# Flamingo layer on one core: the last key tile's two key-sum additions of each head group move from GpSimd to VectorE, and the written orders of all five engines are laid anew

## The reference, cut to what matters

```
xn = layernorm(x)
Q = xn Wq' + bq;  K = ctx Wk' + bk;  V = ctx Wv' + bv          (16 heads of 32)
attn = softmax(Q K' / sqrt(32)) per head;  x1 = x + tanh(g0) (attn V Wo' + bo)
n = layernorm(x1);  probs = softmax(n Rw + rb);  gate = max probs; e = argmax probs  (8 experts)
out = x1 + tanh(g1) * gate * (n Expert[e] + expert_bias[e])
```

## Time and profile before

| | us |
|---|---|
| median of 3 runs | 1189.92 (1188.95 to 1192.12) |
| the profiled execution, its own time | 1192.07 |
| its span, first to last instruction | 1190.3 |
| PE busy / DVE busy / POOL busy / ACT busy | 1094.6 / 759.0 / 667.2 / 563.0 |
| mean granted clock | 0.956 |

### The profile page before, as it was taken

One profiled execution on the slowest core, in us unless ns is written; L12 is line 12 of the kernel. 1 busy time (PEld: TensorE's weight loads), 2 busy tenths in 40 slices (PEclk: granted clock), 3 DMA queues, 4 the chain that ended last, 5 costly groups with the idle time before them and its releaser, 6 DMA issues.

```text
span 1190.3 us, 19122 instructions
## 1 busy us (share of the span) xinstructions
PE 1094.6 (92%) x5464; PEld 709.2 (60%) x5464; DVE 759.0 (64%) x1620; ACT 563.0 (47%) x1016; POOL 667.2 (56%) x446
## 2 busy tenths in 40 slices
PE   2798999999999999999999999999999996898996
PEld 1564467556755675567556655575557642786774
DVE  4645545766576657665765677556765665778654
ACT  4145643564356435644564356445644456423431
...
GB/s 230 62 77 102 82 72 80 113 80 81 79 121 80 81 77 119 82 79 89 111 79 72 79 120 72 73 80 111 86 81 73 83 53 321 127 95 147 166 140 54
DMA packets 70885, 119.39 MB, mean 100 GB/s; under 512 B 17854, under 2 KB 18878, under 8 KB 70656
## 3 DMA queue, kind: packets, MB, share of 16 engines
...
q10 hardware_dynamic: 2048, 0.53, 0.2%
...
## 4 chain that ended last, share of the span: by engine, by line
PE 68%; DVE 13%; issue 6%; ACT 5%; POOL 3%; DMA 3%; DVEq 1%; ACTq 0%; SPq 0%; POOLq 0%
PE jb L459 10%; PE jb L460 9%; PE jb L461 9%; PE sc L482 8%; PE jb L502 8%; PE hb L492 8%; DVE maxima L836 6%; PE sc L664 5%; ACT probs L688 3%; PE jb L602 2%; PE jb L515 2%; POOL psum_keys L1095 2%; PE jb L530 1%; PE jb L594 1%; PE hb L650 1%
## 5 line engine op out<-in xcount | busy, mean ns | idle before, releaser
L836 DVE TENSOR_REDUCE maxima<-jb 128x1 f32<-128x512 f32 x512 | 321.7, 680 | 112.2 <-PE jb L502 110.8
L688 ACT ACTIVATE probs<-sc 128x512 f32<-128x512 f32 x512 | 285.4, 598 | 190.5 <-PE sc L482 153.8
L1095 POOL TENSOR_TENSOR psum_keys<-psum_keys,probs 128x1024 f32<-128x1024 f32 x128 | 302.6, 2384 | 110.7 <-ACT probs L688 110.6
L1095 POOL TENSOR_TENSOR psum_keys<-probs 128x1024 f32<-128x1024 f32 x64 | 151.8, 2383 | 231.3 <-ACT probs L688 230.9
L502 PE MATMUL jb<-k_stack,q_stack 96*128 96x512 f32 x512 | 188.4, 435 | 19.1 <-issue 4.9
L482 PE MATMUL sc<-q_stack,k_stack 98*128 98x512 f32 x512 | 190.7, 435 | 14.9 <-ACT probs L688 11.5
L482 PEld LDWEIGHTS sc<-q_stack,k_stack 98*128 98x128 f32 x512 | 94.4, 192 | 107.6 <-ACT probs L688 56.0
L502 PEld LDWEIGHTS jb<-k_stack,q_stack 96*128 96x128 f32 x512 | 92.6, 190 | 110.4 <-issue 51.2
L492 PE MATMUL hb<-probs,values 128*32 128x512 f32 x1024 | 139.3, 628 | 3.4 <-ACT probs L688 2.5
L459 PE MATMUL jb<-c_hi,wk_hi 128*128 128x512 f32 x128 | 52.4, 409 | 15.4 <-POOL c_lo L1099 15.4
L664 PE MATMUL sc<-e_hi,heads_hi 128*128 x156 | 65.9, 422 | 0.5 <-DVE heads_raw L1067 0.5
...
## 6 DMA issues: line engine op xcount, KB each, us to landing
k_stack<-k_hi SPq DMA_DIRECT2D x256, 64.0 KB, 2.0
q_stack<-q_hi SPq DMA_DIRECT2D x256, 64.0 KB, 2.0
stage<-in_x SPq DMA_DIRECT2D x63, 256.0 KB, 2.9
stage<-in_ctx_t SPq DMA_DIRECT2D x32, 256.0 KB, 3.0
k_stack<-k_lo SPq DMA_DIRECT2D x128, 64.0 KB, 2.0
q_stack<-q_lo SPq DMA_DIRECT2D x128, 64.0 KB, 2.0
e_lo<-in_ew SPq DMA_DIRECT2D x8, 1024.0 KB, 14.0
...
```

The source lines that it names most:

```text
L688: nc.scalar.activation(probs[:, kt % 2, h, :], scs[(16 * g + n) % NSC][:], ACT.Exp, scale=SCALE)\
L836: nc.vector.tensor_reduce(maxima[g % 2][:, n:n + 1], jbs[j][:], AX.X, ALU.max).then_inc(s["mx_done"], 1)
L1095: nc.gpsimd.tensor_tensor(psum_keys[:, two, :], in0, probs[:, kt % 2, two, :], ALU.add)\
```

## The change

The two additions `A4` and `A5` of each of the 32 groups leave GpSimd's table and stand in VectorE's (64 additions of 128x1024 elements in all). The semaphore `acc_done`, which counted a group's six additions, becomes two, `acc_done0` and `acc_done1`, one for each pair of heads, with three counts a group; every wait on it is rewritten to the same data. All tables are written anew. The code part, cut:

```diff
 # tensor_program, SUM
-                    pe.wait_ge(s["acc_done"], 6 * (g + 1))
+                    for i in range(2):
+                        pe.wait_ge(s[f"acc_done{i}"], 3 * (g + 1))
 # scalar_program, E
-                    wait(act, s["acc_done"], 6 * g + (h2 + 1 if kt >= 2 else 2 * kt - 4 + h2 + 1))
+                    wait(act, s[f"acc_done{h2}"], 3 * g + (1 if kt >= 2 else kt - 1))
 # vector_program, A (kt is 3 for A4 and A5)
-                    wait(dve, s["acc_done"], 6 * g + n - 1)
-                    nc.vector.tensor_tensor(psum_keys[:, two, :], psum_keys[:, two, :], probs[:, kt % 2, two, :], ALU.add)\
-                        .then_inc(s["acc_done"], 1)
+                    if kt == 1:
...
+                    else:
+                        wait(dve, s[f"acc_done{h2}"], 3 * g + kt - 1)
+                        in0 = psum_keys[:, two, :]
+                    nc.vector.tensor_tensor(psum_keys[:, two, :], in0, probs[:, kt % 2, two, :], ALU.add)\
+                        .then_inc(s[f"acc_done{h2}"], 1)
 # gpsimd_program, A
-                        wait(pool, s["acc_done"], 6 * g + n - 1)
+                        wait(pool, s[f"acc_done{h2}"], 3 * g + kt - 1)
```

The parts of the tables that the prediction speaks of:

```diff
 OPENING
 "SP"
-        "LW1 ^DC0 ^DC1 ^DC2 LW0 ^DC3 ^DX0 LC LW2 LW3 ^DX1 ^DX2 ^DX3 ^0SK ~RW2 ~RW3 ^0SQ",
+        "^DC0 ^DC1 ^DC2 LW1 ^DC3 ^DX0 LW0 ^DX1 ~RW2 ^DX2 LC ~RW3 ^DX3 LW2 LW3 ^0SK ^0SQ ^1SQ",
 "PE"
-        "^0K ^0Kb ^0Kc ^0Kd ^T4 ^T5 ^T6 ^T7 ^0Q ^0Qb ^0Qc ^0Qd ^0M0 ^0M1 ^0M2 ^0M3 ^0M4 ^0M5 ^V0 ^Vb0 ^1Q ^1Qb",
+        "^0K ^0Kb ^0Kc ^T4 ^0Kd ^T5 ^T6 ^T7 ^0Q ^0Qb ^0Qc ^0Qd ^0M0 ^0M1 ^0M2 ^0M3 CS ^0M4 ^0M5 ^0M6 ^1Q ^1Qb ^1Qc",
 "ACT"
-        "WT0 WT1 WT2 WT3 ^C0 ^C1 TH WT4 ^C2 WT5 ^C3 ^0K ^NX0 WT6 WT7 WT8 WT9 ^T4 WT10 ^NX1 WT11 WT12 ^NX2 ^T5 ^NX3",
-        "WT13 WT14 ^T6 ^T7 WT15 ^0Q ^1Q ^V0 ^0MT ^1K ^0MD ^V1 ^0E0 ^0E1 ^V2 ^0E2 ^0E3 ^0E4 ^0E5 ^0E6 ^0E7 ^0E8 ^2Q",
+        "^C0 ^C1 ^C2 WT0 WT1 WT2 WT3 ^C3 ^NX0 WT4 WT5 ^0K WT6 ^NX1 ^T4 ^NX2 ^T5 ^T6 ^NX3 ^T7 WT7 WT8 WT9 WT10 WT11",
+        "WT12 WT13 WT14 TH ^0Q WT15 ^1Q ^V0 ^0MT ^0MD ^1K ^0E0 ^0E1 ^0E2 ^V1 ^0E3 ^0E4 ^0E5 ^V2 ^0E6 ^2Q ^0E7 ^0E8",
 "DVE"
-        "WT0 WT1 WT2 ^LX0 WT3 WT4 WT5 ^LX1 ^0K ^LX2 ^LX3 ^T4 ^T5 ^T6 ^T7 WT6 WT7 WT8 WT9 WT10 ^0Q ^0M0 ^0M1 ^0M2",
+        "WT0 WT1 WT2 WT3 ^LX0 ^LX1 WT4 WT5 ^LX2 ^LX3 ^T4 ^0K ^T5 ^T6 ^T7 WT6 WT7 WT8 WT9 WT10 ^0Q WT11 WT12 WT13",
 ORDER
 "ACT" (around the start of group 3's exponentials)
-        "~RT3 2E15 3MT 3MD ~RS1 ^0K 2OU 3E0 3E1 3E2 3E3 3E4 2SUM
+        ~RT3 3MT 3MD 3E0 3E1 3E2 ^0K 2OU 3E3 3E4 3E5 2SUM ... ^1Q W0 ^1K ^0MT ^0MD ~RS1
 "DVE" (after the change, in the order of the table)
+        "0A4 1M13 1M14 1M15 1MT 0A5 2M0 2M1 ...
+        ... 2M14 2M15 1A4 2MT ~LI0 ~OP2 ~LR2 0NM ^LX0 1A5 ~OP3 ...
+        ... 3M14 3M15 ^0Q 3MT ~RS1 2A4 2A5 ^0K 2SC ...
+        "^1K ^0MT 3A4 ~RC1 ~RG1 3A5 ^1M0 ^1M1 ^1M2 ^1M3 ~LI1 ^1M4 ^1M5 ^1M6 PA 3SC ^1M7 ^1M8 ^1M9 W0 3NM W1 PC ^2Q",
+        "^2K 3NL ^1M10 W6 OP0 LR0 ^1M11 ^1M12 OP1 W2",
 "POOL"
-        "~LR0 1A0 ^C0 1A1 ^C1 ^C2 ^C3 1A2 ~OP2 ~OP3 1A3 1A4 1A5 ~LR1 ^LX0 ^LX1 2A0 2A1 ^LX2 ^LX3 2A2 2A3 2A4 2A5",
-        "OP0 OP1 3A0 3A1 3A2 3A3 3A4 3A5 ^0A0 ^0A1 ^0A2 ^0A3 ^0A4 GA0 ^0A5",
+        "LX2 LX3 ~2A2 ~2A3 ~3A0 ~3A1 ~3A2 ~OP0 ~3A3 ~OP1 0A0 0A1 0A2 0A3 ~LR0 1A0 ^C0 1A1 ^C1 ^C2 ^C3 1A2 ~OP2 1A3",
+        "~OP3 ~LR1 ^LX0 ^LX1 2A0 2A1",
 CLOSING
 "SP"
-        "~~RW2 ~DR2 W0 ~~RW3 W1 W6 W2 W3 W4 W5 W7 ~DR3 EB ~RW0 ~RW1 ~RW2 ~RW3",
+        "~DR2 W1 ~~RW2 W6 W2 ~~RW3 W3 W4 ~DR3 W5 W7 EB ~RW0 ~RW1 ~RW2 ~RW3",      (W0 now ends ORDER's "^0SK W0 DR0 DR1")
 "DVE"
-        "~LR1 ~OP2 W3 ~RS0 ~OP3 LO0 LO1 ~RG0 W7 LO2 LO3 FI0 ~LR2 ...
+        "~LR1 ~OP2 W3 W7 LO0 ~OP3 ~LR2 LO1 ~RS0 LO2 ~LR3 FI0 ...
 "POOL"
-        "GA1 ~OP2 ~OP3 GA2 GA3 GA4 W4 GA5 ~LR0 W5 GA6 ...
+        "~2A2 ~2A3 ~OP0 ~3A0 ~3A1 ~3A2 ~3A3 GA0 ~OP1 ~LR0 ~OP2 GA1 GA2 GA3 ~OP3 W4 W5 GA4 GA5 SE0 ...
```

More of the change, by code:

```diff
@@ L50 @@
     "SP": [
-        "~~RW2 1SQ 1SK ^DC0 ~~RW3 2SQ 2SK ^DC1 ^DC2 ~RW0 ~RW1 ^DC3 ~DR2 ~DR3 ^DX0 3SQ ^DX1 3SK ^DX2 ^DX3 DR0 DR1",
-        "^0SQ ^0SK",
+        "1SK ~~RW2 ~~RW3 ^DC0 2SQ 2SK ~RW0 ^DC1 ^DC2 ^DC3 ~DR2 ~DR3 ~RW1 ^DX0 3SQ ^DX1 3SK ^DX2 ^DX3 ^0SQ ^0SK W0",
+        "DR0 DR1 ^1SQ",
     ],
     "PE": [
[11 rows of a table removed]
[11 rows of a table added]
     ],
     "ACT": [
[6 rows of a table removed]
[6 rows of a table added]
     ],
     "DVE": [
[6 rows of a table removed]
[6 rows of a table added]
     ],
     "POOL": [
-        "~LR0 1A0 ^C0 1A1 ^C1 ^C2 ^C3 1A2 ~OP2 ~OP3 1A3 1A4 1A5 ~LR1 ^LX0 ^LX1 2A0 2A1 ^LX2 ^LX3 2A2 2A3 2A4 2A5",
-        "OP0 OP1 3A0 3A1 3A2 3A3 3A4 3A5 ^0A0 ^0A1 ^0A2 ^0A3 ^0A4 GA0 ^0A5",
+        "LX2 LX3 ~2A2 ~2A3 ~3A0 ~3A1 ~3A2 ~OP0 ~3A3 ~OP1 0A0 0A1 0A2 0A3 ~LR0 1A0 ^C0 1A1 ^C1 ^C2 ^C3 1A2 ~OP2 1A3",
+        "~OP3 ~LR1 ^LX0 ^LX1 2A0 2A1",
     ],
@@ L90 @@
     "SP": [
-        "LW1 ^DC0 ^DC1 ^DC2 LW0 ^DC3 ^DX0 LC LW2 LW3 ^DX1 ^DX2 ^DX3 ^0SK ~RW2 ~RW3 ^0SQ",
+        "^DC0 ^DC1 ^DC2 LW1 ^DC3 ^DX0 LW0 ^DX1 ~RW2 ^DX2 LC ~RW3 ^DX3 LW2 LW3 ^0SK ^0SQ ^1SQ",
     ],
     "PE": [
[5 rows of a table removed]
[5 rows of a table added]
     ],
     "ACT": [
[3 rows of a table removed]
[3 rows of a table added]
     ],
     "DVE": [
[4 rows of a table removed]
[3 rows of a table added]
     ],
     "POOL": [
-        "^C0 ^C1 ^C2 ^C3 ^LX0 ^LX1 ^LX2 ^LX3 ^0A0 ^0A1 ^0A2 ^0A3 ^0A4 ^0A5",
+        "^C0 ^C1 ^C2 ^C3 ^LX0 ^LX1",
     ],
@@ L117 @@
     "SP": [
-        "~~RW2 ~DR2 W0 ~~RW3 W1 W6 W2 W3 W4 W5 W7 ~DR3 EB ~RW0 ~RW1 ~RW2 ~RW3",
+        "~DR2 W1 ~~RW2 W6 W2 ~~RW3 W3 W4 ~DR3 W5 W7 EB ~RW0 ~RW1 ~RW2 ~RW3",
     ],
     "PE": [
[3 rows of a table removed]
[3 rows of a table added]
         "Y20 TO22 Y21 TO23 Y22 TO24 Y23 TO25 Y24 TO26 Y25 TO27 Y26 TO28 Y27 TO29 Y28 TO30 Y29 TO31 Y30 TO32 Y31",
@@ L369, in build @@
             "w_lo_done", "p_const", "d_const", "p_init", "a_const", "cs_mm", "rw_done",
-            "st_done", "exp_done", "acc_done", "pv_done", "ms_done", "mx_done", "mt_mm", "mt_hi", "mt_lo",
+            "st_done", "exp_done", "acc_done0", "acc_done1", "pv_done", "ms_done", "mx_done", "mt_mm", "mt_hi", "mt_lo",
             "max_rows_in", "sum_mm", "sum_used", "sc_mm", "sc_used", "wide_done", "nm_mm", "nm_hi", "ou_done", "nm_chain", "nm_done",
@@ L828, in item @@
                     wait(dve, s["exp_done"], 16 * g + HG * kt + 2 * h2 + 2)
-                    wait(dve, s["acc_done"], 6 * g + n - 1)
-                    nc.vector.tensor_tensor(psum_keys[:, two, :], psum_keys[:, two, :], probs[:, kt % 2, two, :], ALU.add)\
-                        .then_inc(s["acc_done"], 1)
+                    if kt == 1:
+                        wait(dve, s["sum_mm"], g)
+                        wait(dve, s["w_lo_done"], 3 * NF)
+                        in0 = probs[:, 0, two, :]
+                    else:
[3 more added lines that the diff above has]
+                        .then_inc(s[f"acc_done{h2}"], 1)
                 elif kind == "M":
@@ L1014, in item @@
                     wait(dve, s["pv_done"], NT * NG * B)
-                    wait(dve, s["acc_done"], 6 * NG * B)
+                    for i in range(2):
+                        wait(dve, s[f"acc_done{i}"], 3 * NG * B)
                     wait(dve, s["rc_free"], 2 * B)
@@ L1128, in item @@
                     wait(pool, s["pv_done"], NT * NG * B)
-                    wait(pool, s["acc_done"], 6 * NG * B)
+                    for i in range(2):
+                        wait(pool, s[f"acc_done{i}"], 3 * NG * B)
                     wait(pool, s["fin"], n + 1 - SLOTS)
```

## The result

The changed kernel takes 1199.37 us (median of 4 runs, 1198.33 to 1203.3) against 1189.43 us for the kernel before beside it: ratio 1.0086, 95% interval 1.0058 to 1.0115. It is slower by about 10 us, in these runs. I had forecast 1171 us and faster; 1199.4 also lies outside my range of 1160 to 1187. The rival priced at 1200 us, (c), is the one that came.

What follows compares the result with a forecast made beforehand. TensorE, busy 92% of the span, was taken as the bound, with up to 11 us slack a batch; 1192.07 - 9.0 - 0 - 6.7 - 3.0 = 1173.4 us profiled, less 2.15, say 1171 us; range 1160 to 1187.

Steps and rivals of the forecast that it cites:

- (c): Body: moved additions on the maxima's path each wait for a whole GpSimd instruction, 3.6 us; 1229 or 1200 us; chance 0.11.
- part 2: Body: 64 additions moved from GpSimd to VectorE, 1.21 us each, change nothing since SUM is not waited for: 0 us.
- the bank rotation: Body: the four banks of TensorE's M, taken to cover delays of VectorE's maxima behind moved additions; no gain or loss booked.
- Part 1: Opening: reordered loads and splits start Q and the first M earlier, and the gain stays: -9.0 us, bounds -5.5 to -10.5.
- Part 3: Body: new orders remove TensorE's 0.96 us wait before group 3's fourth S in seven batches: -6.7 us; other moves zero.
- Part 4: Last group's tail and closing: LR1 ahead of expert splits -4.65, W1 and PC +1.6; net -3.0 us, bounds +4 to -10.

Runs made afterwards that it cites:

- e2: The changed kernel's orders with all A4 and A5 additions put back on GpSimd, each behind its A3 (or the OP3 or OP1 that follows): ratio 0.9833.
- e1: The changed kernel with one VectorE addition, 1A4, moved from in front of 2MT, OP2 and 0NM to behind them: 1175.7 us, ratio 0.9755.
- the small kernels: Four kernels without the model, only VectorE instructions meeting GpSimd rows: VectorE let in behind one GpSimd instruction, 3.27 us for every row length in the first.
- e4: The kernel before with only the changed kernel's opening, up to 0Q, on SyncE, TensorE, ScalarE and VectorE: ratio 0.9932.

## Why the prediction was wrong

**The step that failed** is part 2, "the moved additions, in the body: 0", with its price of a meeting as "a whole GpSimd addition", 1.21 + 2.39 = 3.6 us. Measured, it is two terms. Seven of the eight additions of a batch are as priced, 1.22 us where I had 1.21 from interpolation, and well placed the eight bring 6.9 us in six batches (e2 to e1) where I booked nothing: I had written that SUM is not waited for, and behind the new orders it is (e2, e1). The eighth, 1A4, costs 31.5 us in the same stretch (changed kernel to e1): 4.56 us a batch of excess on VectorE, after which TensorE stands 4.03 us, and then a stretch at 1.2 GHz.

Rival (c) had the kind of mechanism and nearly the sum, 1200, and both are partly luck. It put the place at 0A4, "directly in front of 1M13"; it was 1A4, which I had listed as standing "in front of 2MT" and covered by the bank rotation. The rotation covers the maxima; it does not cover OP2, whose bank 0NM needs. And (c) counted one GpSimd instruction over eight batches; it was three over six.

A row that shows more than one instruction was in the trace of before, and I read another. I took the 4.82 us of L915 as a meeting with one subtraction. It began at 1019.96, before that subtraction (1020.16), while GpSimd was at an indirect DMA, so it is no clean price of one instruction. Such a price was there five times: in five steady batches the same 0.17 us step took 1.54 to 1.61 us (the first at 234.15) and ended with the GpSimd addition that it had met, which had nothing behind it. And 40 us earlier a 128x2 step of VectorE with a median of 0.23 us waited for both of GpSimd's stage additions, the one it met and the next. VectorE and POOL of the kernel before:

```profile
978.31 2.26 DVE L944 TENSOR_SCALAR row<-rt,tiny 128x2 f32<-128x2 f32 x1
```

```profile
968.74 9.34 POOL L1095 TENSOR_TENSOR psum_keys<-psum_keys,probs 128x1024 f32<-128x1024 f32 x4 [2.24 <-ACT probs L688]
978.04 2.50 POOL L1119 TENSOR_TENSOR stage<-stage,gbo 128x512 f32<-128x512 f32 x2
```

It asked 0.27 us into the first and ended at 980.57, with the second (980.54). With that row, and with GpSimd's new queue read as "OP2 1A3 OP3" behind 1A2, the price could have been had: 1.28 + 2.39 + 1.26 - 0.2 + 1.1 = 5.8 us. By the opening's row above it could as well have been one instruction; no row said which.

The Trainium skill (SBUF — State Buffer, SBUF: two separate sides) says of a VectorE instruction with two SBUF inputs and a GpSimd one that reads SBUF that whichever starts first gets the shared pair of ports for the whole instruction. Read so that the other goes next, 1A4 would have been let in at 341.04 and ended near 342.2; the trace of the changed kernel disagrees (345.73), while the small kernels agree with it to 0.1 us.

**Part 1**, -9.0, was mis-sized: -6.1 to the first M (37.07, not 34) and -5.2 at the sixth MT. Q starts at 26.86, not 24.4: Wk, issued at 2.17 behind three tiles, landed after 7.7 us, so the first matmul came at 11.35, and two more waits of 2.0 and 3.07 us stand before T's transposes. By my own mark, a first M after 38, it is not wrong, only short. By e4, with the opening alone, it is -0.7% [0.4, 1.0], about -8 us.

**Part 3**, -6.7 for the new orders: the number came, not the working. The wait of 0.96 us before L482 is gone (0.22 in its place), and e2 against e4 gives 6.9 us in six batches. But e2 has the SUM wait of 1.78 us a batch instead, and no less idle time in all; the gain is in busy time that I had not priced. That the two numbers agree is luck. The bounds of 3 us a batch hold.

**Part 4**, -3.0, came as +0.6, of two opposite pieces. Up to the first expert matmul 6.3 us were won (from the last MT 69.1 us before, its own start being 1043.27, and 62.8 after); from there to the end the changed kernel took 154.0 us against 147.0. My marks were 20 to 23 us to the last SUM (it is 24.3) and 31 from the first output matmul to the first expert one (32.1). I put no cause to the second: the same closing orders as before took 147.0 us in one trace and 165.3 in another (e4), so this stretch moves by more than the difference. On e4's chip the new closing orders took 162.5 (e1) and 159.4 (e2), no longer than the old.

**The sum** against the traces: forecast -9.0 + 0 - 6.7 - 3.0 = -18.7. With the measured values it is -5.2 (opening), then -6.9 (orders), -6.9 (additions) and +31.5 (1A4) in the six batches, -5.0 in the groups behind them, which I had not forecast apart, and +0.6 behind the last MT: +8.1 against the measured +6.3, the rest being 1.9 us by which e4's and the old kernel's six batches differ with the same orders.
